# First operation of half the gate and up tiles and of the third weight on GpSimd, twelve places for up, third weight's sums started in the first stage

## The reference, cut to what matters

```python
# attention: 16 heads of 64, grouped linear layers (8 groups of 128)
qkv  = grouped_linear(x, w_qkv)
out  = softmax(q * k^T / 8) v                # over 2048 keys
out  = grouped_linear(out, w_proj) + b_proj
x    = layernorm(x + out)
# feed forward, inner width 4096, all three weights ternary
def weight_quant(w):
    scale = 1 / clip(mean(abs(w)), 1e-5)     # mean over the whole weight
    return clip(round(w * scale), -1, 1) / scale
def act_quant(x):                            # per token, 8 bits
    scale = 127 / clip(max(abs(x)), 1e-5)
    return clip(round(x * scale), -128, 127) / scale
h    = silu(act_quant(x) @ weight_quant(w_gate)) * (act_quant(x) @ weight_quant(w_up))
x    = layernorm(x + act_quant(h) @ weight_quant(w_down))
```

## Time and profile before

| | us |
|---|---|
| time, median of 3 runs | 1289.52 (1288.72 to 1291.1) |
| the profiled execution, its own time | 1290.59 |
| its span on the slowest core (core 4) | 1289.0 |
| spans of the 8 cores | 1278.8 to 1289.0 |
| PE busy | 1149.7 (89% of the span) |
| DVE busy | 911.7 (71%) |
| ACT busy | 616.9 (48%) |
| POOL busy | 117.4 (9%) |

### The profile page before, as it was taken

How to read it: one execution, slowest core, us unless ns; L and a number is a source line. 1 busy time by engine, 2 the same in 40 slices (tenths; PEclk the granted TensorE clock), 3 DMA queues, 4 the chain that set the end, 5 groups by cost and what they waited for, 6 DMA issues and landing times.

```text
span 1289.0 us, 17877 instructions; the slowest of 8 cores (1278.8 to 1289.0 us)
## 1 busy us (share of the span) xinstructions
PE 1149.7 (89%) x6465; PEld 455.1 (35%) x6502; DVE 911.7 (71%) x1797; ACT 616.9 (48%) x679; POOL 117.4 (9%) x146
## 2 busy tenths in 40 slices
PE   3888998884898886599999999999999999999997
PEld 0333333321333222233333333333444444444443
DVE  4878889977899874474664547353789777977774
ACT  3798998884454487555555555554011111110110
POOL 1222112220001000010010001000000000000000
PEclk8999999997899898799999999999999999999999
DMA  8999934569799757242323223020523333233313
GB/s 237 307 326 316 325 102 158 176 195 318 239 250 226 208 138 241 90 92 65 92 70 78 86 39 117 5 70 1 145 89 81 89 82 99 72 89 66 82 34 82
DMA packets 129031, 179.74 MB, mean 139 GB/s; under 512 B 90033, under 2 KB 90801, under 8 KB 128946
## 3 DMA queue, kind: packets, MB, share of 16 engines
q1 hardware_dynamic: 120050, 149.52, 41.1%
q0 software_dynamic: 8896, 29.08, 7.4%
HBM read 127.41 MB, written 30.93 MB: 123 GB/s over the span
## 4 chain that ended last, share of the span: by engine, by line
PE 66%; DVE 13%; DMA 12%; ACT 5%; issue 4%; SPq 0%; POOL 0%; DVEq 0%; ACTq 0%; POOLq 0%
PE ps L802 32%; PE ps L897 16%; DMA stage<-wu 6%; PE ps L553 6%; PE ps L571 6%; PE ps L578 5%; ACT P L559 4%; DMA stage<-wd 3%; DVE asum L417 2%; DVE G L434 1%; ACT G L430 1%; DMA stage<-wg 1%; DMA stage<-xT 1%; DVE wgq L440 1%; DVE h L814 1%
## 5 line engine op out<-in xcount | busy, mean ns | idle before, releaser
L559 ACT ACTIVATE P<-ps 128x1024 bf16<-128x1024 f32 x512 | 492.5, 1021 | 236.6 <-PE ps L553 234.9
L808 ACT ACTIVATE T<-ps,tsc 128x512 f32<-128x512 f32 x128 | 88.0, 687 | 376.3 <-PE ps L802 330.5
L802 PE MATMUL ps<-wgq,xqT 128*128 128x512 fp8e4 x1024 | 249.2, 383 | 15.2 <-DVE hm L840 5.2
L802 PE MATMUL ps<-wuq,xqT 128*128 128x512 fp8e4 x1024 | 250.0, 384 | 8.7 <-DVE h L814 8.6
L897 PE MATMUL ps<-wdq,hqT 128*128 128x512 fp8e4 x1024 | 229.9, 380 | 1.3 <-DVE wdq L440 1.3
L571 PE MATMUL ps<-P,onesb 128*64 128x512 bf16 x1024 | 206.3, 399 | 14.2 <-DVE DT L594 14.2
L553 PE MATMUL ps<-Q,K 64*128 64x512 bf16 x1024 | 175.0, 389 | 44.1 <-ACT P L559 34.7
L578 PE MATMUL ps<-P,V 128*64 128x512 bf16 x1024 | 199.9, 386 | 0.9 <-DVE RC L598 0.5
L802 PEld LDWEIGHTS ps<-wuq,xqT 128*128 128x128 bf16 x1024 | 97.0, 99 | 142.0 <-issue 35.3
L802 PEld LDWEIGHTS ps<-wgq,xqT 128*128 128x128 bf16 x1024 | 95.8, 98 | 144.9 <-issue 39.9
L897 PEld LDWEIGHTS ps<-wdq,hqT 128*128 128x128 bf16 x1024 | 97.4, 98 | 129.8 <-issue 17.8
(11 more groups left out here) (95 smaller groups left out, 703.1 us busy)
## 6 DMA issues: line engine op xcount, KB each, us to landing
stage<-wu SPq DMA_DIRECT2D x64, 512.0 KB, 12.2
stage<-wd SPq DMA_DIRECT2D x58, 512.0 KB, 5.5
stage<-wg SPq DMA_DIRECT2D x42, 512.0 KB, 19.1
stage<-xT SPq DMA_DIRECT2D x16, 512.0 KB, 13.6
XB<-x SPq DMA_DIRECT2D x16, 512.0 KB, 5.3
xp_s<-XB SPq DMA_DIRECT2D x16, 512.0 KB, 2.6
Y<-xp_s SPq DMA_DIRECT2D x16, 512.0 KB, 4.3
y<-Y SPq DMA_DIRECT2D x16, 512.0 KB, 2.6
```

The lines of the kernel that those rows point to most:

```text
L559: exp_tok[i] = act.do(lambda e: e.activation(P_sb[i % 4][:, :], bank(sb, 2), AF.Exp, bias=-C0, scale=0.125), pv_tok.get(i - 4), t)
L802: tp = pe.do(lambda e, ic=ic, w=w, bk=bk: e.matmul(bank(bk), xqT[b][:, ic, :], W_sb[w][:, 8 * q + ic, sl], start=(ic == 0), stop=(ic == 7) ...
L808: ta = act.do(lambda e: e.activation(T[:, :], bank(gb), AF.Tanh, bias=0.0, scale=tsc[:, t:t + 1]), tp, T_free[k], sc_tok[t])
```

## The change

The diff, without the lines in which only a name changes:

```diff
-    AT = alloc("AT", [128, 8, 128], BF16)[0]
+    AT = [alloc(f"AT{i}", [128, 7, 128], BF16)[0] for i in range(2)]
...
-    G1 = [alloc(f"G1{i}", [128, 1024], I8)[0] for i in range(2)]
+    G1 = [alloc(f"G1{i}", [128, 1024], I8)[0] for i in range(4)]
...
-    RB = [alloc(f"RB{i}", [128, 512], F32)[0] for i in range(2)]
+    RB = alloc("RB", [128, 512], F32)[0]
...
-    order += [("tern", 1, k, k % 8, True) for k in range(16)]
-    order += [("tern", 0, k, k % 8, True) for k in range(22, 24)]
+    ring = list(range(8)) + [18, 19, 20, 21]
+    order += [("tern", 1, k, ring[k % 12], True) for k in range(16)]
+    order += [("tern", 0, 22, 4, True), ("tern", 0, 23, 5, True)]
...
-    ring = [0, 1] + list(range(22, 30))
     rest = [k for k in range(32) if not 8 <= k < 14]
-    order += [("sum", 2, k, ring[n % 10], True) for n, k in enumerate(rest)]
+    order += [("sum", 2, k, n % 8, True) for n, k in enumerate(rest)]
...
-            if hold[0] and w == 2:
+            if hold[0] and s_ >= 22:
                 return
...
             if kind == "sum":
+                while second:
+                    yield limit()
...
-            b = g1_n[0] % 2
+            b = g1_n[0] % 4
             g1_n[0] += 1
-            if w == 2:
-                t = act.do(lambda e, w=w, src=src, b=b: e.activation(
-                    G1[b][:, :], src[:, :], AF.Identity, bias=0.0, scale=wst[:, 8 * w + 2:8 * w + 3]),
-                    g1_tok[b], t_stat[w], load_tok.get(o))
-            else:
-                t = dve.do(lambda e, w=w, src=src, b=b: e.tensor_scalar(
-                    G1[b][:, :], src[:, :], wst[:, 8 * w + 2:8 * w + 3], 1.0, ALU.mult, ALU.min),
-                    g1_tok[b], t_stat[w], load_tok.get(o))
+            own = w < 2 and b % 2 == 1
+            t = (dve if own else pool).do(lambda e, w=w, src=src, b=b: e.tensor_scalar(
+                G1[b][:, :], src[:, :], wst[:, 8 * w + 2:8 * w + 3], 1.0, ALU.mult, ALU.min),
+                g1_tok[b], t_stat[w], load_tok.get(o))
             used(o, t)
-            yield 0.05 if w == 2 else 0.8, None
-            extra = t_qkv_last[0] if w == 2 else None
-            g1_tok[b] = dve.do(... the second operation, at once ...)
-            t_tern[(w, k)] = g1_tok[b]
-            yield 0.75, None
+            if own:
+                yield 0.8, None
+            second.append((w, k, b, t))
+            if len(second) > 2:
+                yield limit()
+        while second:
+            yield limit()
+    second = deque()
+    def limit():
+        w, k, b, t = second.popleft()
+        g1_tok[b] = dve.do(lambda e: e.tensor_scalar(
+            W_sb[w][:, k, :], G1[b][:, :], -1.0, 1.0, ALU.max, ALU.min, saturate=False),
+            t, t_qkv_last[0] if w == 2 else None)
+        t_tern[(w, k)] = g1_tok[b]
+        return 0.75, None
...
-            pace = 0.55 if 0 not in t_red else 0.75 if ast[0] < 230 else 0.95
+            pace = 0.62 if 0 not in t_red else 0.72
...
-    for i in range(0, 256, 2):
+    for i in range(0, 252, 2):
...
             load_at(0)
+            load_at(1)
+        if i == 230:
+            hold[0] = False
+            for s_ in range(22, 30):
+                stage_tok[s_] = t_qkv_last[0]
+            load_more()
         if i in (242, 244):
             proj_half(0, i // 2 - 121)
+            if i == 244:
+                load_at(2)
...
     while bg:
         bgstep(1.0)
-    load_at(1)
-    hold[0] = False
-    for s_ in range(22, 30):
-        stage_tok[s_] = t_qkv_last[0]
-    load_more()
...
                 load_tile(t + 1)
-                if t + 1 != 8:
-                    load_at(t + 1)
+                if t + 2 < 16 and (t + 2) // 8 == t // 8:
+                    load_at(t + 2)
...
                 if t == 0 and oc == 7:
+                    while 2 not in t_red:
+                        credit[0] = 1.0
+                        weight_step(credit)
...
-            need_weights(2, 31)
+            if t == 0:
+                for k in range(32):
+                    need_weights(2, k)
```

More of the change, by code:

```diff
@@ L145, in build @@
     AO7 = alloc("AO7", [128, 1024], BF16)[0]
-    AT = alloc("AT", [128, 8, 128], BF16)[0]
-    blo, _ = alloc("blo", [128, 1024], BF16, at=off[0] - 2048)
+    AT = [alloc(f"AT{i}", [128, 7, 128], BF16)[0] for i in range(2)]
+    blo, _ = alloc("blo", [128, 1024], BF16, at=off[0] - 3584)
     b3, _ = alloc("b3", [128, 1024], BF16)
@@ L328, in build @@
     t_red = {}
-    g1_tok = [None, None]
+    g1_tok = [None] * 4
     g1_n = [0]
@@ L425, in weight_ops @@
                 continue
-            b = g1_n[0] % 2
+            b = g1_n[0] % 4
             g1_n[0] += 1
-            if w == 2:
-                t = act.do(lambda e, w=w, src=src, b=b: e.activation(
-                    G1[b][:, :], src[:, :], AF.Identity, bias=0.0, scale=wst[:, 8 * w + 2:8 * w + 3]),
-                    g1_tok[b], t_stat[w], load_tok.get(o))
-            else:
-                t = dve.do(lambda e, w=w, src=src, b=b: e.tensor_scalar(
-                    G1[b][:, :], src[:, :], wst[:, 8 * w + 2:8 * w + 3], 1.0, ALU.mult, ALU.min),
-                    g1_tok[b], t_stat[w], load_tok.get(o))
-            used(o, t)
-            yield 0.05 if w == 2 else 0.8, None
-            extra = t_qkv_last[0] if w == 2 else None
-            g1_tok[b] = dve.do(lambda e, w=w, k=k, b=b: e.tensor_scalar(
-                W_sb[w][:, k, :], G1[b][:, :], -1.0, 1.0, ALU.max, ALU.min, saturate=False), t, extra)
-            t_tern[(w, k)] = g1_tok[b]
-            yield 0.75, None
+            own = w < 2 and b % 2 == 1
+            t = (dve if own else pool).do(lambda e, w=w, src=src, b=b: e.tensor_scalar(
+                G1[b][:, :], src[:, :], wst[:, 8 * w + 2:8 * w + 3], 1.0, ALU.mult, ALU.min),
+                g1_tok[b], t_stat[w], load_tok.get(o))
+            used(o, t)
+            if own:
[13 more added lines that the diff above has]
+        return 0.75, None
     later = []
@@ L600, in norm @@
         t3 = dve.do(lambda e: e.transpose(
-            RB[b][:, :].rearrange("r (k c) -> r k c", c=32),
-            RC[:, :].rearrange("r (k c) -> r k c", c=1).broadcast_to([128, 16, 32])), t2, u_free[b])
+            RB[:, :].rearrange("r (k c) -> r k c", c=32),
+            RC[:, :].rearrange("r (k c) -> r k c", c=1).broadcast_to([128, 16, 32])), t2, u_free[1 - b])
         def mult():
@@ L606, in mult @@
                 ao7_tok[qc] = u_free[b] = pool.do(lambda e: e.tensor_tensor(
-                    AO7[:, 512 * qc:512 * qc + 512], U_sb[b][:, :], RB[b][:, :], ALU.mult),
+                    AO7[:, 512 * qc:512 * qc + 512], U_sb[b][:, :], RB[:, :], ALU.mult),
                     pool.sem.tok(), t3, u_done_of[u], ao7_free[qc])
@@ L611, in mult @@
             t4 = u_free[b] = pool.do(lambda e: e.tensor_tensor(
-                AO[b][:, :], U_sb[b][:, :], RB[b][:, :], ALU.mult),
+                AO[b][:, :], U_sb[b][:, :], RB[:, :], ALU.mult),
                 pool.sem.tok(), t3, u_done_of[u], ao_free[b])
@@ L685, in load_at @@
         b = t % 2
-        atl_tok[t] = pool.dma(sem(f"atl{b}"), AT[:, 0:7, :], at_s[t, :, 0:7, :], at_free[0],
+        atl_tok[t] = pool.dma(sem(f"atl{b}"), AT[b][:, :, :], at_s[t, :, 0:7, :], at_free[b],
                               *[at_tok[(p, t // 4)] for p in range(7)])
@@ L723, in proj_half @@
             g = 4 * hf + j
-            src = AT[:, g, :] if g < 7 else AO7[:, 128 * (t % 8):128 * (t % 8) + 128]
+            src = AT[b][:, g, :] if g < 7 else AO7[:, 128 * (t % 8):128 * (t % 8) + 128]
             tp = pe.do(lambda e, g=g, j=j, src=src: e.matmul(
@@ L735, in proj_half @@
             return
-        at_free[0] = tp
+        at_free[b] = tp
         if t == 3 or t == 7:
@@ L1005, in need_weights @@
                 run_later(force=True)
+                while totals:
+                    totals.pop()(7)
+            assert not wdone[0] or (w, k) in t_tern
     for kind, t in seq:
@@ L1017, in build @@
                 load_at(8)
+                load_at(9)
             proj_half(t, 0)
```

## The result

| | before | after |
|---|---|---|
| median | 1289.12 us (1288.64 to 1291.1, 4 runs) | 1382.2 us (1381.8 to 1384.47, 4 runs) |
| ratio | | 1.0723, 95% interval 1.0704 to 1.0741 |
| profiled execution: own time, span | 1290.59, 1289.0 | 1384.47, 1382.9 |

The forecast was 1269.5 us, the range 1238 to 1300: the sign is wrong and the time lies far outside. Of the rivals, the long operation on GpSimd names the cause, but it was priced at 1303 to 1323. In some executions, whatever the kernel, one die shows a lower granted clock and takes some per cent longer; the ratios and comparisons here leave these out.

A forecast was written before the change was run, and what follows sets the result against it. DVE was taken to bound from 177 to 438 us. GU1 ending 12 us later, then GU2 and D0 in 73 us for 108, gave -23; attention steps +3: -20 from 1290.6, less 1.1, is 1269.5 us, range 1238 to 1300.

The forecast's parts named there:

- the long operation on GpSimd: Rival: GpSimd's new operation takes 2.1 us, giving 1303 us, or 2.7 us, giving 1323; chance 0.18.
- I take 1.04 for the new one, which also has one input.: GpSimd's new first operation was taken at 1.04 us, like the cast of `xT`, with 2.7 as far end.
- 32 x (0.63 + 0.38) us for each us: How DVE's loss, first stage and GU1, grows with GpSimd's operation length: 32 us for each us.
- 0.65 us for each of the 32 in the first stage.: DVE's loss to each GpSimd operation there; with 0.4 each in GU1, 21 + 13 = 34 us.
- 0.7 of GpSimd's time: Share of a GpSimd operation for which DVE stands still: 0.96 us for each 1.34 us multiplication.
- The order: 11 tiles and 10 sums of down move ahead of GU0; all down tiles fall into GU1.
- The DVE ledger, 266 us: DVE's busy time from the sums' end to GU1's end: 24 + 45 + 22 + 36 + 105 + 34.
- GU2 and D0 at PE's pace, 73 us: With no weight left PE sets the pace there: 73 us in place of 108.
- I take 16 in all: DVE's idle time from the sums' end to GU1's end: 16 us, 8 of it around down's reloads.
- the sums' end, 168 us: The weights' last sum, during attention, was put at 168 us, between 160 and 176; before, 175.5.
- the gain is eaten: Rival: full lock costs DVE 12 us more and reloads stall GU1 14 us, not 8: 1288 us; chance 0.10.
- Edits costed at nothing.: ACT losing 32 operations, `AT` doubled and `RB` single were put at 0, twelve places for up at 0 to -3 us.

The follow-up runs named there:

- micro: A separate kernel timing GpSimd operations on 128x1024 float32 alone and beside DVE's; the change's form took 3.76 us, a cast 1.08.
- one_op: The changed kernel with the minimum of 1 dropped from GpSimd's operation, leaving one arithmetic step: 1348.1 us, ratio 1.0465 to the kernel before.
- cast: The changed kernel with GpSimd's multiplication replaced by a plain cast to int8, scale left out: 1287.17 us, ratio 0.9978 to the kernel before.
- no_pool: The changed kernel with gate's and up's first operations all on DVE and down's on ACT: 1297.89 us, ratio 1.0077 to the kernel before.
- at2: The kernel before with only AT double-buffered, its loads one tile earlier, and RB single: 1287.88 us, ratio 0.9998.
- no_pool_ring: no_pool with sums of down in places 0, 1, 22 to 29 and no flush before GU0's last block: 1273.17 us, ratio 0.9879 to the kernel before.
- quarter: no_pool_ring with every fourth gate and up tile's first operation on GpSimd: 1288.68 us, ratio 1.0002 to the kernel before.

## Why the prediction was wrong, step by step

1. **"I take 1.04 for the new one, which also has one input."** This is the step that failed. The operation takes 3.76 us alone (micro) and 4.03 in the changed kernel, far above the 1.7 that the prediction itself named as its sign of being wrong; with a cast in its place, and nothing else changed, the time is 1287 us and not 1382. The choice between 1.04 and 2.7 went by the number of inputs, and both rows were of other kinds of instruction: a cast, and a two-input multiplication. What sets the time is the kind of instruction and its number of steps, which micro shows in one row each. The mean of the two nearest rows would have been wrong as well; right would have been to say that no row shows a `tensor_scalar` on this engine, and to leave its upper end open.
2. **The rival was priced on DVE alone.** "32 x (0.63 + 0.38) us for each us" lets a long operation cost what it takes from DVE. At 4.03 us it gives 1269.5 + 32 x 1.01 x 2.99 = 1366; measured are 1382. That it comes near is chance: both of its terms are far from what was measured (point 3), and missing is the check that comes before any lock, whether 64 operations fit beside the stretch at all. The question to ask was at what duration POOL becomes the bound. In GU1 there are 60 us for 32 operations, 1.9 us each; between the sums' end and GU0, 150 us less some 30 of POOL's other work, for 32, 3.75 us each. 4.03 is above both. At 1.9 us the bound is passed in GU1, and from there on GU1 grows by 32 us for each us, which one_op shows (23.4 us for 24).
3. **"0.65 us for each of the 32 in the first stage."** With an operation of 1.04 the sum of both places is right, 35 us in cast for 34, but by luck: gate's and up's three groups hold 29 of it where 21 were forecast, down's 6 where 13 were. With the long one a first operation on DVE loses 1.15 - 0.78 = 0.37 us and the two second ones 0.42 and 0.35 over 0.69, together 1.1 for each operation on GpSimd, not 0.63 of 4.03 = 2.5 (against no_pool's means it is 1.0). The loss hardly grows with the instruction: in micro 0.7 us for a cast of 1.34, 1.1 for an operation of 4.4 to 4.7. "0.7 of GpSimd's time" was a ratio read from one duration, and was used as a law.
4. **The order**: right. 11 sums of down start ahead of GU0 in cast and in the changed kernel; 10 were forecast. **The DVE ledger, 266 us**: right, 264.88 in cast. **GU2 and D0 at PE's pace, 73 us**: right in both, 73 and 75. The rule was sound: once no weight is left, PE sets the pace.
5. **"I take 16 in all" of idle time**: 33 in cast. And **the sums' end, 168 us**: 171 in cast; in the changed kernel the last sum starts at 173.7. Both were too hopeful, together 20 us, as large as the forecast gain. This second error was hidden by the first. It is the rival "the gain is eaten", by waits and not by the lock: with the duration assumed, that rival's 1288 us would have been the result (1287.17), half by luck, since its extra 12 us of lock did not come.
6. **Edits costed at nothing.** `AT` doubled: 0, right (at2, 0.9998). But its gain of 9 us was also counted among the idle time that goes, and there it was not worth 9 either, since a wait of 7.34 us took its place. What the prediction put inside the order or at 0 to -3 (the places, the early release, the late second operation, the paces) holds the whole gain of 16 us that no_pool_ring shows without GpSimd. And the flush at the last block of GU0, which it didn't look at, costs 25 us as soon as gate and up stay on DVE (no_pool against no_pool_ring); in cast and in the changed kernel PE has no such gap, so there it was rightly at nothing, by luck.

The Trainium skill's warning (Perfetto Trace Analysis, Optimizing Scalar/DVE Operations) is that a move between DVE and GpSimd may bring nothing, because of the shared port. The runs bear out that it brings nothing: 0.78 us saved, 1.09 paid (quarter). Its stricter sentence (SBUF — State Buffer, Who interferes with whom) is that the loser waits for the whole instruction. That isn't borne out: beside GpSimd operations of 4.4 to 4.7 us DVE ran one every 1.05, the longest 1.64.

## What to carry to other kernels

Before work moves to an engine, find a row of that very operation on that engine, and if there is none, measure it alone first: a neighbour of the same size and number of inputs was off by 3.6 times. Then ask two questions in this order: do all moved operations fit in the time beside which they stand, and what does each cost the engine it relieves. An engine's share of the whole span (27% here) answers neither. And when a change joins several edits, cost the dull ones by themselves too: here they held the gain. A control that moves work back can also shift the order of everything else, as no_pool did; changing only the length of the instruction, as cast did, kept the order.

## What the runs showed of the hardware

- On GpSimd, 128x1024 from f32: cast 1.08 us, `tensor_scalar` with one step 2.83, with two 3.68, whether to bf16 or int8; with the scale from SBUF 0.08 more. On 512 columns 2.06, so by a straight line through the two some 0.36 us would be fixed (an estimate).
- GpSimd's `tensor_scalar` and DVE's first and second operations slow each other: 4.4 to 4.7 us for 3.70, and 1.05 for 0.78 and 1.01 for 0.72. GpSimd casts beside the same cost DVE some 0.7 us each (6 first operations in 7.52 us for 4.68, beside 4 casts), and took 1.34 for 1.08. DVE's reduction took 1.22 us with or without GpSimd beside it, and GpSimd 3.77 beside it for 3.76 alone: neither slowed the other.
